# Two self-attentions with 64 keys: turning two heads' probabilities as one block, values as 64x32 tiles, and the causal mask as a bf16 product

## What is computed

```python
# stage 3
scores = jnp.einsum('bhqd,bhkd->bhqk', q, k) / jnp.sqrt(jnp.float32(dh))
attn = jax.nn.softmax(scores, axis=-1)
ctx = jnp.einsum('bhqk,bhkd->bhqd', attn, v)
# stage 5
scores = jnp.einsum('bqhd,bkhd->bhqk', q, k) * SCALE
causal = jnp.triu(jnp.ones((S, S), dtype=bool), k=1)
scores = jnp.where(causal[None, None], -1e+30, scores)
attn = jax.nn.softmax(scores, axis=-1)
out = jnp.einsum('bhqk,bkhd->bqhd', attn, v).reshape(B, S, D)
```

## Time and profile before

| | |
|---|---|
| median of three runs | 2927.6 us (2924.82 to 2930.02) |
| the profiled execution's own time | 2923.03 us |
| its span in the trace | 2921.1 us |
| mean granted TensorE clock | 0.977 of full |
| TensorE (PE) busy | 2763.2 us, 95% |
| VectorE (DVE) busy | 1208.8 us, 41% |
| ScalarE (ACT) busy | 981.5 us, 34% |
| GpSimd (POOL) busy | 287.2 us, 10% |

### The profile page before, as it was taken

The page is one execution under the profiler, slowest core; times in us unless marked ns, Lnnn a source line. Parts: engine busy times, 40 slices in busy tenths (PEclk is TensorE's granted clock), DMA queues, the critical chain, the costliest instruction groups (busy, mean ns, idle before and its releaser), DMA issues.

```text
span 2921.1 us, 41179 instructions
## 1 busy us (share of the span) xinstructions
PE 2763.2 (95%) x18162; PEld 1959.6 (67%) x18177; DVE 1208.8 (41%) x1822; ACT 981.5 (34%) x1468; POOL 287.2 (10%) x279
## 2 busy tenths in 40 slices
PE   8989999998999899999999998999999999998798
PEld 3447347356677578888888876788778878863433
DVE  4364344356742533333333343433442443344611
ACT  3242223124443344443434332423432442431310
POOL 1110110212003000000000001111011011000000
PEclk9999999999999999999999999999999999999899
DMA  8963984961012122222222220001001101013198
GB/s 351 379 245 134 379 347 186 362 247 71 15 72 87 44 111 92 101 101 88 100 101 94 94 94 32 30 34 48 27 23 48 40 12 46 26 66 130 45 420 356
DMA packets 61969, 385.56 MB, mean 132 GB/s; under 512 B 6192, under 2 KB 10544, under 8 KB 32352
## 3 DMA queue, kind: packets, MB, share of 16 engines
q1 hardware_dynamic: 27072, 190.58, 17.0%
q0 software_dynamic: 29776, 188.15, 16.7%
q10 hardware_dynamic: 4944, 4.20, 0.4%
HBM read 377.64 MB, written 5.26 MB: 131 GB/s over the span
## 4 chain that ended last, share of the span: by engine, by line
PE 78%; DVE 8%; DMA 4%; ACT 2%; POOL 1%; issue 1%; ACTq 0%; DVEq 0%; POOLq 0%
PE PS L445 11%; PE PS L446 11%; PE PS L447 11%; PE PS L311 4%; PE PS L1878 3%; PE PS L1895 3%; PE PS L645 3%; PE PS L1896 3%; PE PS L1897 3%; PE PS L1880 3%; PE PS L1879 3%; PE PS L1937 3%; PE PS L618 2%; PE PS L1916 2%; DMA PR<-in_ctxN 2%; DVE T L1345 2%
## 5 line engine op out<-in xcount | busy, mean ns | idle before, releaser
L2114 DVE TENSOR_TENSOR RB<-PS,rows 128x512 f32<-128x512 f32 x104 | 72.0, 692 | 392.5 <-PE PS L1897 392.5
L445 PE MATMUL PS<-H_high,W_high 128*128 128x512 f32 x576 | 224.7, 390 | 2.1 <-DVE rstd L1561 2.1
L445 PE MATMUL PS<-X_high,W_high 128*128 128x512 f32 x576 | 224.5, 390 | 1.3 <-DVE X_low L1254 1.3
L446 PE MATMUL PS<-H_low,W_high 128*128 128x512 f32 x576 | 224.8, 390 | 0.0
L447 PE MATMUL PS<-H_high,W_part 128*128 128x512 f32 x576 | 224.7, 390 | 0.0
L447 PE MATMUL PS<-X_high,W_part 128*128 128x512 f32 x576 | 224.1, 389 | 0.0
L446 PE MATMUL PS<-X_low,W_high 128*128 128x512 f32 x576 | 224.1, 389 | 0.0
L1201 DVE TENSOR_TENSOR W_part<-ring,W_high 128x2048 fp32r<-128x2048 f32 x63 | 147.0, 2334 | 185.0 <-ACT W_high L1197 185.0
L1197 ACT ACTIVATE W_high<-ring 128x2048 fp32r<-128x2048 f32 x72 | 137.0, 1914 | 252.4 <-PE PS L447 252.4
L1240 DVE TENSOR_TENSOR H_low<-T,H_high 128x512 fp32r<-128x512 f32 x144 | 99.4, 690 | 206.2 <-ACT H_high L1227 206.2
L2019 ACT ACTIVATE RC<-PS,vec 128x384 f32<-128x384 f32 (+2 forms) x128 | 76.3, 596 | 298.4 <-PE PS L1880 298.4
(11 more groups left out here) (397 smaller groups left out, 5512.0 us busy)
## 6 DMA issues: line engine op xcount, KB each, us to landing
ring<-in_experts SPq DMA_DIRECT2D x83, 1024.0 KB, 4.8
ring<-in_tiles SPq DMA_DIRECT2D x39, 1024.0 KB, 4.8
RC<-in_ctxN POOLq DMA_DIRECT2D x24, 1536.0 KB, 10.9
RA<-in_ctxT POOLq DMA_DIRECT2D x20, 1536.0 KB, 7.2
T<-in_ctxN POOLq DMA_DIRECT2D x24, 1024.0 KB, 15.9
RA<-in_ctxT POOLq DMA_DIRECT2D x12, 1666.0 KB, 14.1
RB<-in_ctxT POOLq DMA_DIRECT2D x12, 1666.0 KB, 15.7
RB<-in_ctxT POOLq DMA_DIRECT2D x12, 1536.0 KB, 10.7
```

What stands on the lines that cost most here:

```text
L445: pe.matmul(ps, a, xh, start=start, stop=False)
L446: pe.matmul(ps, a, xl, start=False, stop=False)
```

## The change

The block-diagonal layout goes. Probabilities are normalised in place with one instruction on 128 partitions, and the scores are kept so that two heads of the same group stand side by side (`pairs5`: 128 query rows by 2 heads x 64 keys). One turn of such a 128x128 block gives the keys of head `gp = 0` on partitions 0 to 63 and of head `gp = 1` on 64 to 127, with the queries of both batches as columns. So a pair needs 8 turns and two copies out. A value product now has 64 rows (one head's keys), 32 value columns and 64 queries (one batch). The values of batch `u` stand on partitions `64 u` and up, though, and the keys of head `gp` on `64 gp` and up, so a copy of the values with its halves swapped (`VSWAP`, two ScalarE instructions for a pair, L1439 and L1440) serves where `u` and `gp` differ. The 32 products go to banks 6 (`gp = 0`) and 7 (`gp = 1`). In stage 5 the mask is cast to bf16 (L2261) and multiplied by the identity into banks 0 to 3 ahead of the scores of each pair, which then accumulate on it. There are four buffers of `raw5` and two of `PT`. The order of the streams in stages 3 and 5 is written anew. In the list of stage 6's homes the buffer RA4[0], which held `probs`, may be filled after an earlier step.

```diff
-            home6 += [(RA4[0], "spare_loaded5", "s5.at.T3.3"), (ring[slot["s5.wo"]][:, :, :], f"weights_loaded{slot['s5.wo']}", "s5.wo.used")]
+            home6 += [(RA4[0], "spare_loaded5", "s4.v3.3"), (ring[slot["s5.wo"]][:, :, :], f"weights_loaded{slot['s5.wo']}", "s5.wo.used")]
...
+            if masked:
+                pe.wait_ge(*at.done("s5.causal"))
+                for a in range(G):
+                    pe.matmul(PS[:, a, 0:KC * S], idb[:, :], causal_bf, start=True, stop=False)
             for g in range(KC):
                 for a in range(G):
                     r = slice(a * HD, (a + 1) * HD)
                     for u in (0, 1):
                         m = slice((2 * bp + u) * S, (2 * bp + u + 1) * S)
-                        mm = pe.matmul(PS[u * S:(u + 1) * S, a, g * S:(g + 1) * S], Q[r, g, m], K[r, g, m], start=True, stop=True)
+                        mm = pe.matmul(PS[u * S:(u + 1) * S, a, g * S:(g + 1) * S], Q[r, g, m], K[r, g, m], start=not masked, stop=not masked or g == KC - 1)
...
+        def turn_pe(pe, at, tag, bp):
+            pe.wait_ge(*at.done(f"{tag}.p{bp}"))
+            for half in (0, 1):
+                k = 4 + half
                 if bank_reader.get(k):
                     pe.wait_ge(*at.done(bank_reader[k]))
+                for j in range(4):
+                    mm = pe.transpose(PS[:, k, j * P:(j + 1) * P], pairs5[bp][:, 4 * half + j, :], C["ident"])
+                mm.then_inc(*at.step(f"{tag}.T{bp}.{half}"))
+                bank_reader[k] = f"{tag}.T{bp}.{half}.out"
+
+        def weigh_pe(pe, at, tag, V, bp):
+            for k in (6, 7):
+                if bank_reader.get(k):
+                    pe.wait_ge(*at.done(bank_reader[k]))
+            for half in (0, 1):
+                pe.wait_ge(*at.done(f"{tag}.T{bp}.{half}.out"))
+            pe.wait_ge(*at.done(f"{tag}.swap{bp}"))
+            for g2 in (0, 1):
+                for u in (0, 1):
+                    for a in range(G):
+                        for gp in (0, 1):
+                            h = G * (2 * g2 + gp) + a
+                            r = slice(gp * S, (gp + 1) * S)
+                            of = V if u == gp else VSWAP
+                            mm = pe.matmul(PS[a * HD:(a + 1) * HD, 6 + gp, g2 * P + u * S:g2 * P + (u + 1) * S], of[r, bp, h * HD:(h + 1) * HD],
+                                           probsT[bp % 2][r, 2 * a + g2, u * S:(u + 1) * S], start=True, stop=True)
...
+            def swap(bp):
+                act.wait_ge(*at.done(f"{v_tag}.{bp}.out"))
+                act.activation(VSWAP[0:S, bp, :], V[S:P, bp, :], ACT.Copy).then_inc(*at.step())
+                act.activation(VSWAP[S:P, bp, :], V[0:S, bp, :], ACT.Copy).then_inc(*at.step(f"{tag}.swap{bp}"))
...
-                for u in (0, 1):
-                    r = slice(u * S, (u + 1) * S)
-                    dve.tensor_tensor(probs[bp % 2][r, :, r], x[r, :, :], sm[r, :].unsqueeze(2).broadcast_to([S, H, S]), ALU.mult).then_inc(*at.step(f"{tag}.p{bp}"))
+                dve.tensor_tensor(x, x, sm.unsqueeze(2).broadcast_to([P, H, S]), ALU.mult).then_inc(*at.step(f"{tag}.p{bp}"))
```

More of the change, by code:

```diff
@@ L1420, in values_of, with attn_act @@
             mm.then_inc(*at.step(f"{tag}.O{bp}"))
-            bank_reader[7] = f"{tag}.O{bp}.out"
-        def attn_act(act, at, tag):
+            bank_reader.update({6: f"{tag}.O{bp}.out", 7: f"{tag}.O{bp}.out"})
+        def attn_act(act, at, tag, V, v_tag):
             def exps(bp):
                 act.wait_ge(*at.done(f"{tag}.sub{bp}"))
[L1426 to L1437, removed]
@@ L1439, in attn_dve, with turned_out @@
-        def attn_dve(dve, at, tag, O, mask, values):
+                act.activation(raw5[bp], raw5[bp], ACT.Exp, scale=HD ** -0.5).then_inc(*at.step(f"{tag}.exp{bp}"))
+            def swap(bp):
+                act.wait_ge(*at.done(f"{v_tag}.{bp}.out"))
+                act.activation(VSWAP[0:S, bp, :], V[S:P, bp, :], ACT.Copy).then_inc(*at.step())
+                act.activation(VSWAP[S:P, bp, :], V[0:S, bp, :], ACT.Copy).then_inc(*at.step(f"{tag}.swap{bp}"))
+            def turned_out(bp):
+                if bp >= 2:
+                    act.wait_ge(*at.done(f"{tag}.O{bp - 2}"))
+                for half in (0, 1):
+                    act.wait_ge(*at.done(f"{tag}.T{bp}.{half}"))
+                    act.activation(PT[bp % 2][:, half * 512:(half + 1) * 512], bank(4 + half), ACT.Copy).then_inc(*at.step(f"{tag}.T{bp}.{half}.out"))
@@ L1441, in maxima, with attn_dve @@
+            return exps, swap, turned_out
+        def attn_dve(dve, at, tag, O):
             def maxima(bp):
-                x, m = raw5[bp % 2], peak[bp % 2]
+                x, m = raw5[bp], peak[bp % 2]
                 ps = PS[:, 0:G, 0:KC * S].rearrange("p a (g k) -> p a g k", k=S)
                 dve.wait_ge(*at.done(f"{tag}.S{bp}"))
[L1445 to L1454, removed]
@@ L1461, in normalise @@
             def normalise(bp):
-                x, sm = raw5[bp % 2], sums[bp % 2]
+                x, sm = raw5[bp], sums[bp % 2]
                 dve.wait_ge(*at.done(f"{tag}.exp{bp}"))
@@ L1695, in s3_act @@
             linear_out(act, at, "s3.k", (0, 1, 2, 3), range(KC), lambda ps, c: act.activation(K3[:, c, :], ps, ACT.Identity, bias=v("bqkv", 4 + c)))
-            attn_act(act, at, "s3.at")
+            exps, swap, turned_out = attn_act(act, at, "s3.at", V3, "s3.v")
+            exps(0)
+            swap(0)
+            exps(1)
+            swap(1)
+            exps(2)
+            turned_out(0)
+            swap(2)
+            turned_out(1)
+            exps(3)
+            swap(3)
+            turned_out(2)
+            turned_out(3)
             expert_high(act, at, MOE(0), 0)
@@ L1729, in s3_dve, with values_in @@
                 dve.tensor_tensor(X3L[:, c, :], X3[:, c, :], X3H[:, c, :].bitcast(FP32), ALU.subtract).then_inc(*at.step(f"s3.x3.low{c}"))
-            attn_dve(dve, at, "s3.at", O3, False, lambda bp: values_dve(dve, at, "s3.v", V3, "bv3", (4, 5, 6), (bp,)))
+            maxima, normalise, out = attn_dve(dve, at, "s3.at", O3)
+            def values_in(bp):
+                values_dve(dve, at, "s3.v", V3, "bv3", (6, 7), (bp,))
+            maxima(0)
+            values_in(0)
+            maxima(1)
+            normalise(0)
+            values_in(1)
+            maxima(2)
+            normalise(1)
+            values_in(2)
+            maxima(3)
+            values_in(3)
+            normalise(2)
+            out(0)
+            normalise(3)
+            out(1)
+            out(2)
+            out(3)
             expert_low(dve, at, MOE(0), 1)
@@ L2220, in s5_act @@
             linear_out(act, at, "s5.k", (4, 5, 6, 7), range(KC), lambda ps, c: act.activation(K5[:, c, :], ps, ACT.Identity, bias=v("bk5", c)))
-            attn_act(act, at, "s5.at")
+            exps, swap, turned_out = attn_act(act, at, "s5.at", V5, "s5.v")
+            exps(0)
+            swap(0)
+            exps(1)
+            swap(1)
+            turned_out(0)
+            exps(2)
+            swap(2)
+            turned_out(1)
+            exps(3)
+            swap(3)
+            turned_out(2)
+            turned_out(3)
         def s5_dve(dve, at):
@@ L2228, in s5_dve @@
             values_dve(dve, at, "s5.v", V5, "bv5", (0, 1, 2, 3))
-            attn_dve(dve, at, "s5.at", O5, True, lambda bp: None)
+            dve.tensor_copy(causal_bf, causal.rearrange("p g k -> p (g k)")).then_inc(*at.step("s5.causal"))
+            maxima, normalise, out = attn_dve(dve, at, "s5.at", O5)
+            maxima(0)
+            maxima(1)
+            normalise(0)
+            maxima(2)
+            normalise(1)
+            out(0)
+            maxima(3)
+            normalise(2)
+            out(1)
+            normalise(3)
+            out(2)
+            out(3)
             for c in range(KC):
```

86 lines of the change are left out of this document (28 added, 58 removed).

## The result

| | before | after |
|---|---|---|
| median | 2928.05 us (4 runs, 2924.82 to 2930.02) | 2913.71 us (4 runs, 2908.84 to 2916.01) |
| profiled execution, its span | 2923.03, 2921.1 | 2915.3, 2913.5 |
| mean granted clock | 0.977 | 0.976 |

A forecast was written before the change was run, and what follows sets the result against it. VectorE's passes over 128x1024 elements were taken to bound both self-attentions. Stage 5's -8.1, stage 3's -5.7 and +2.6 for the lower clock sum to -11.2, from 2927.6 to 2916.4 us; range 2909 to 2923.

The forecast's parts named there:

- Passes: VectorE passes removed in both attentions: 9.8 us less for stage 5's four pairs, 4.9 us less in stage 3.
- Stage 3: Stage 3's attention: -4.9 for passes, -1.3 for waits on value projections, +0.5 for the tail, together -5.7 us.
- my tail: Stage 3, last normalisation to projection: turn, two rounds of products and copy-outs, 4.6 us against 4.05, +0.5.
- Stage 5: Stage 5's attention at full clock: -9.8 + 0.3 + 0.45 + 1.45 - 0.5 = -8.1 us.
- the one on the clock: Lower TensorE clock in stage 5's last round: turns +0.7, products +0.4, projection +1.5, together +2.6 us; ends 0 and 5.
- (c): Stage 5: VectorE waits once, before the second maximum, for mask 0.45, scores 0.90 and two handoffs: 1.45 us.
- cast and first mask product: Stage 5, before the first scores: mask cast on VectorE 0.3 us, first bf16 mask product on the path 0.45.
- The projection's +1.5: Stage 5's projection: its first matmuls run at half speed for 3 us, costing 1.5 us.
- A waiting VectorE over 4 us in either stretch: Sign of being wrong: a waiting VectorE holds over 4 us in stage 3's or stage 5's attention.
- C: Slower rival: the value products' row halves do not run side by side, 7.2 us a pair, 2954.6 us; chance 0.04.
- Covers: ScalarE's swap and other copies, 3.5 us a pair against VectorE's 5.8, hide beside VectorE's work; normalisations cover the swap.
- D: Rival: the clock stays high in both attentions, -13.8 us, 2913.8 us; chance 0.15.

The follow-up runs named there:

- e1_halves: The changed kernel with the normalisation as two half-height instructions on 64 partitions again; 2923.04 us in one run.
- f1_fill: The changed kernel with 36 filler products in TensorE's waits in stage 5's attention; median 2916.1 us, 5 runs, ratio 0.9958.
- g0_after: The changed kernel run again without any edit, on another comparison's chip; median 2913.36 us, 6 runs, ratio 0.9954.
- e3_no_swap: The changed kernel without the half-swapped copy, all value products reading unswapped values; 2912.3 us in one run.
- f4_home_late: The changed kernel with RA4[0] filled only after the last turn of stage 5's last pair, as before; median 2919.09 us, 7 runs, ratio 0.9975.
- g1_combined: The changed kernel with fillers in both stages and stage 3's pair 2 products in banks 0 and 1, before pair 3's turn; median 2907.98 us, ratio 0.994.
- h1_before_fill: The kernel before the change with 42 fillers in TensorE's waits in stage 5's attention; 2925.11 us in one run.
- e2_mask_dve: The changed kernel with stage 5's mask added by VectorE again, without cast and bf16 mask product; 2916.82 us in one run.
- f2_only3: The change in stage 3 alone, stage 5 and the RA4[0] step as in the kernel before; median 2924.82 us, 10 runs, ratio 0.9986.

## Why the prediction was right

**The bound.** It was VectorE's passes: e1_halves puts them back, and most of the gain goes. The durations that I took for instructions of the same shape held: 1224 for the full-height normalisation, maxima straight from PSUM 1220.

**Passes, a little too small.** I priced a removed pass by its own 1.22 us. What counts is start to start. The timelines of before and after, of two half-height passes with the next instruction and of the one full-height pass with the next:

```profile
977.85 2.47 DVE L1474 TENSOR_TENSOR RC<-RB,misc 64x1024 f32<-64x1024 f32 x2
980.42 1.23 DVE L1455 TENSOR_REDUCE misc<-PS 128x16 f32<-128x1024 f32 x1
```

```profile
981.78 1.22 DVE L1470 TENSOR_TENSOR RB<-RB,misc 128x1024 f32<-128x1024 f32 x1
982.92 0.68 DVE L1497 TENSOR_TENSOR T<-PS,rows 128x512 f32<-128x512 f32 x1
```

2.57 us against 1.14: the half pass was worth 1.43 here, and 1.25 to 1.42 at the other pairs of stage 3, not 1.22.

**Stage 3: -7.6 where I had -5.7.** Waits apart, VectorE's work up to the end of the last normalisation went from 29.93 us to 23.51, 6.4 less. The normalisations make 5.4 of it, where I had 4.9. One copy-out makes 0.6: pair 1's now lies in the tail, beside TensorE, which my tail counted and my passes did not. The last 0.4 are gaps between other instructions. VectorE's waits fell from 2.77 to 1.30 us, 1.5 where I had 1.3. The tail grew from 4.1 (1000.30 to 1004.40) to 4.4 (998.19 to 1002.59), by 0.3 instead of 0.5. 6.4 + 1.5 - 0.3 = 7.6.

**Stage 5: -5.8 where I had -7.0** (-8.1, and 1.1 for the clock). The step that failed is the one on the clock: I put the lower level into the last round alone. It was there from the second mask product on, with the full clock back only for pair 1's turn and products and pair 2's turn (1.14, 0.85 and 1.09 us). The second scores made VectorE wait 2.35 us where (c) said 1.45; at the full clock, in f1_fill, it was 1.55. And the first products, behind slow scores of pair 3 and a slow turn (1.97 instead of 1.09), held up the copy-out by 0.79, which I had at nothing. The passes gave 0.7 more than I had (10.5 for 9.8), by the same start-to-start reading; the tail took 4.9 where I had 4.65. The first maximum starts 1.83 us after the value additions, against 1.08 before, so cast and first mask product cost 0.75 together, as stated. At the full clock (f1_fill) the attention gave 8.4, where I had 8.1.

The premise of that step was wrong by my own prices. I gave TensorE about 2 us of work in each 5.9 and called it less than before. But 0.45 for the mask, 0.90 for scores, 1.1 for the turn and 0.95 for products make 3.4. Measured, TensorE is busy for 18.60 of 31.6 us, 59%, where it was 20.98 of 37, 57%, in the kernel before. So the share of work did not fall, and yet the granted clock went from 0.72 to 0.67. What TensorE did before the first drop can be read, though: the second mask product, already at the lower level, stands behind a wait of 2.58 us for the subtraction, and with fillers in that wait the level stayed up.

The projection's +1.5 was a guess: no row that I named has the 3 us at half speed. The changed kernel's trace has 1.6, but the same projection cost 3.0 in g0_after, so the agreement is luck. Behind it the first products of stage 6 cost 0.4 more as well, which the sum had at nothing.

The misses of the two stages, 1.9 us one way and 1.2 and 0.5 the other, nearly cancel: -11.4 in the trace for -11.2. That the sum is so near is luck too. Against the median's 14.3 the forecast is 3.1 us short, just within the interval (11.1 to 18.2). What is left is in none of the stretches that the change touches, and I do not claim it.

**The signs I had set.** Stage 5 was to take 30.5 us and took 31.56, stage 3 32 and took 30.16. "A waiting VectorE over 4 us in either stretch" was badly set: VectorE waits 4.6 us in stage 3 (0.94 for the first scores, 1.30 for values, 2.36 in the tail) and 8.1 in stage 5, but in stage 3 of the kernel before it already waited 6.4. By its letter the sign would have called the bound wrong, and e1_halves shows that it was right. **C** named the two row halves and priced products with no tile beside another, 7.2 us; two halves one after the other would be 1.9 by the same 0.95. The 0.85 measured refutes both.

**Covers.** The swap is covered (e3_no_swap), and the home edit is worth nothing (f4_home_late). The turned copies are covered but for the last (0.61 us in the chain of the tail), which the sum had at 0.6. Value products took 0.85 for my 0.95. On changes of mode, the Trainium skill, "TensorEngine Tiling (Array Packing)", Key Properties, says that they drain the array. In the trace the scores' first record starts at 2689.31, while the last mask record ends at 2689.38: a drain, if it is there, is not to be seen in these rows, whose ends are modelled. The same page of the Trainium skill, Gotcha 1: PSUM Pressure, says that two row tiles may not access one bank together; here they have banks 6 and 7, and the 0.85 gives no sign of one in the other's way. No run put both in one bank.

**D.** The full clock in both stages did not come by itself in either trace of the changed kernel. f1_fill and g1_combined show what it gives.

## What to carry to other kernels

Price VectorE's passes by columns and from start to start: 64 partitions by 1024 columns took 1220 ns and 128 partitions 1224, so the same work on all partitions at once halves it. When the covering engine's work is taken away, price what was under it again, at TensorE's lower clock, and with it the next dense stretch, which starts at the speed that the stretch before left. Fillers in the waits of such a stretch are worth trying where TensorE has just become the late one, and worth nothing (h1_before_fill) as long as another engine covers it. And judge small edits by their stretch in the trace, with its granted clock beside it, since the whole time moves by several us. Take a second trace of the unedited kernel first: here stage 3's attention repeated to 0.1 us and stage 5's to 0.2, but the projection behind stage 5 only to 1.4.

## What was not expected of the hardware

TensorE's instructions of stage 3's attention in the changed kernel ran at three granted clocks. It was 1.00 in the changed kernel's trace and in those of e2_mask_dve and g0_after, 0.94 in f1_fill and f4_home_late, and 0.86 in f2_only3, with 30.16, 30.4 and 31.7 us. In the last three the level falls at the same place, in pair 2's turn, behind the same wait of 1.78 us for its normalisation that stands in the first three too. In f2_only3 it cost 3.9 us with the projection. What decides it stays open: the three kernels differ from the changed one only in the code of stage 5 and in the table of stage 6's homes. The one long run of g0_after (2923.33, mean clock 0.973, against 0.976 or 0.977 in its others) may be of this kind; it left no trace.

Parting the two row halves of the value products costs 0.13 us at the full clock and 0.36 at the lower one. The shape of the tile made little difference: 64 records on eight tiles take 0.85 us as value products (64x32) and 0.90 as scores (32x64).
